# Attention row maxima turned by one VectorE block transpose a batch and taken ten heads ahead

## Chip, core and metric

The kernel runs on one core of one Trainium2 chip. The metric is the device time of one execution in microseconds (us), the median of the runs of that kernel. The engines are named as the profile names them: PE is TensorE's matmul and PEld its weight load, DVE is VectorE, ACT is ScalarE, POOL is GpSimd, SP is SyncE, which only issues transfers here.

## What is computed

One post-norm transformer layer on `x[32, 256, 128]`, 32 batches of 256 tokens. The attention has 16 heads of 8 features and a bias that falls linearly with the distance of query and key; the feed-forward part has four layers of width 512.

```python
def attention(x):                                   # wq, wk, wv, wo: 128 x 128
    q, k, v = heads(x @ wq.T), heads(x @ wk.T), heads(x @ wv.T)     # [32, 16, 256, 8]
    a = einsum('bhqd,bhkd->bhqk', q, k) / sqrt(8)
    a = softmax(a + slopes[h] * -abs(key - query), axis=-1)
    return merge(einsum('bhqk,bhkd->bhqd', a, v)) @ wo.T + bo

def ffn(x):                                         # ternary weights, scaled by column
    h = silu(lin(x, w1)) * lin(x, w2)
    h = gelu(lin(h, h1)); h = gelu(lin(h, h2))
    return lin(h, w3)

x = layernorm(x + attention(x)); x = layernorm(x + ffn(x))
```

## The kernel before

**Two parts.** `attention` works through the 32 batches, `ffn` through 16 chunks of 512 tokens after it. Only the attention part is touched. Every engine runs its own program in a fixed order, and semaphores tie them together. A step `t` stands for a batch; it has 16 slots `k`, one for each head. The program of every engine is laid out step by step and slot by slot, from step -4 to step 33.

**Each score matrix is made twice.** The softmax needs the maximum of each row before its exponent. So PE first computes the scores of a head with queries on the partitions into a bank `ps_a` (L464), and DVE takes the negated row maxima from it (L762, 128 rows x 2 blocks of queries) into `neg_sb`. Later PE computes the same scores with keys on the partitions into a bank `ps_b` (L472), with the maxima fed in as two more rows of the query operand `qk_stack`, and ACT takes the exponent into `probs` (L654). One slot does both for different heads: head `k` of batch `t` for the exponent, and for the maxima the head that stands `AHEAD = 4` heads further on (`a_slot`). In slots 0 to 11 of step `t` that is head 4 to 15 of batch `t + 1`, in slots 12 to 15 it is head 0 to 3 of batch `t + 2`. A slot's twelve matmuls (four L464, four L472, four of L479, which add the bias where query and key blocks meet) are called a **round** here.

**The way of a maximum.** The maxima have to come back as rows. After eight heads PE transposes half of `neg_sb` by a matmul with the identity into a `ps_b` bank (`turn_max`, L534), ACT copies 16 rows from it to `max_f` (`copy_max`, L630), POOL splits them into two bf16 parts `mrow` (`split_max`, L825 and L827), and SP sends each part into `qk_stack` (`max_rows`, L373). PE waits for that (`m_landed`) at slot 0 for heads 0 to 7, and at slot 8 for heads 8 to 15.

**What stands between the rounds.** The table `AT` says after which slot's round PE does what else: `wo` (L548) and `v` (L540) project, `turn o` (L562) transposes the attention output of the batch before into a `ps_a` bank, `turn norm` (L570) its normalised form into a `ps_b` bank, `qk` (L579) projects queries and keys of batch `t + 4`, and `pv 0` to `pv 3` (L523) multiply four heads' probabilities with the values. DVE has the row maxima in slot order and between them `add_residual` (L713), `take_stats` (L719), `normalise` (L743, L746) and `sum_stats` (L724).

**The banks.** All uses of `ps_a` take three banks in turn, in the order of the list `A_USES`: the 16 rounds with `wo` and `turn o` between them, 18 uses a step. A use waits until the one three places ahead of it in that list has been read: for a round's bank that is `max_done`, the end of DVE's reduction of that round. The uses of `ps_b` take four banks in the same way (`B_USES`, 21 a step, `max 0` and `max 1` among them), and wait for ACT's reading of the one four places ahead.

**The start.** Steps -4 to -1 fill the pipeline: there are projections and maxima, but no exponents before slot 0 of step 0. The maxima of batch 0 begin in slot 12 of step -2.

## Time and profile before

| | |
|---|---|
| median of 3 runs | 802.08 us (801.79 to 804.29) |
| profiled execution, its own time | 799.74 us |
| its span, first to last instruction | 797.9 us |
| busy PE, DVE, ACT, POOL | 96%, 79%, 77%, 39% of the span |
| attention part | about the first 440 us of the span |
| mean granted TensorE clock | 0.995 of full speed |

The span is 1.8 us shorter than the execution's own time, and that execution is 2.3 us below the median. The busy shares are means over two parts with different limits; the attention part is to be read by itself. In the timeline an instruction's matmuls overlap, so what a step of PE costs is the distance of its start from the start of the next, not its duration. The same holds for DVE's and ACT's instructions where they stand back to back.

### The profile page before, as it was taken

How to read it: one execution, taken by the hardware profiler on the slowest of the kernel's cores; microseconds unless marked ns; L12 is line 12 of the kernel's file. 1: busy time of each engine (PE TensorE's matmuls, PEld its weight loads, DVE VectorE, ACT ScalarE, POOL GpSimd, SP SyncE). 2: the span in 40 equal slices, each digit the busy share in tenths (PEclk: the TensorE clock that was granted, in tenths of full speed). 3: DMA queues.
4: the chain of work that ended last, by engine and by line, in shares of the span. 5: the costliest groups of instructions: out<-in, count | busy, mean ns of one | idle time of the engine just before them, and what ended most of it. 6: DMA issues, size and time to landing. Idle time of an engine off the chain costs nothing.

```text
span 797.9 us, 26869 instructions
## 1 busy us (share of the span) xinstructions
PE 769.2 (96%) x10370; PEld 557.4 (70%) x10370; DVE 630.1 (79%) x1303; ACT 611.7 (77%) x1096; POOL 313.4 (39%) x490
## 2 busy tenths in 40 slices
PE   4999999999999999999999999999999999999995
PEld 2566666666666666666665788888888888888873
DVE  4789899899989999989993767777777776666774
ACT  5588787888888888878878777777777777777762
POOL 5346878787756657575634200000000000000001
PEclk9999999999999999999999999999999999999998
DMA  6755565656556565564621100111111111101001
GB/s 181 190 145 166 168 185 159 195 151 182 164 159 166 141 181 136 170 174 144 174 65 44 41 27 28 39 41 39 39 39 39 31 34 39 39 26 40 16 26 54
DMA packets 107341, 81.37 MB, mean 102 GB/s; under 512 B 11168, under 2 KB 94112, under 8 KB 107232
## 3 DMA queue, kind: packets, MB, share of 16 engines
q1 hardware_dynamic: 105632, 76.59, 34.1%
q0 software_dynamic: 880, 2.88, 1.3%
q8 instruction: 79, 1.29, 0.7%
q10 hardware_dynamic: 720, 0.36, 0.2%
q14 instruction: 30, 0.25, 0.1%
HBM read 45.72 MB, written 33.55 MB: 99 GB/s over the span
## 4 chain that ended last, share of the span: by engine, by line
PE 92%; DVE 2%; DMA 2%; issue 2%; ACT 1%; POOL 1%; SPq 0%; POOLq 0%; ACTq 0%; DVEq 0%
PE ps_b L951 17%; PE ps_b L954 17%; PE ps_o L523 15%; PE ps_a L464 11%; PE ps_b L472 6%; PE ps_b L579 4%; PE ps_a L951 3%; PE ps_a L954 3%; PE ps_a L548 2%; PE ps_a L479 2%; PE ps_b L540 2%; PE ps_a L562 2%; PE ps_b L479 2%; PE ps_b L570 1%; PE ps_b L534 1%
## 5 line engine op out<-in xcount | busy, mean ns | idle before, releaser
L762 DVE TENSOR_REDUCE neg_sb<-ps_a 128x2 f32<-128x512 f32 x512 | 324.7, 681 | 37.1 <-PE ps_a L479 29.7
L654 ACT ACTIVATE probs<-ps_b 128x512 f32<-128x512 f32 x512 | 281.4, 591 | 57.2 <-PE ps_b L479 57.1
L464 PE MATMUL ps_a<-qk_stack 52*64 52x256 bf16 x2048 | 178.0, 281 | 5.6 <-DMA qk_stack<-qk_scratch 2.8
L472 PE MATMUL ps_b<-qk_stack 54*64 54x256 bf16 x2048 | 172.3, 276 | 1.1 <-ACT probs L654 0.9
L1062 ACT ACTIVATE gelu_f<-ps_b,sc 128x512 f32<-128x512 f32 x124 | 85.5, 690 | 74.0 <-PE ps_b L954 66.4
L464 PEld LDWEIGHTS ps_a<-qk_stack 52*64 52x64 bf16 x2048 | 82.5, 108 | 79.4 <-DVE neg_sb L762 61.0
L523 PE MATMUL ps_o<-probs,v_aug 128*32 128x256 f32 x2048 | 137.3, 385 | 0.0
L1224 POOL TENSOR_SCALAR vareps_f<-meanvar_f 128x4 f32<-128x4 f32 x15 | 9.7, 644 | 301.0 <-DVE meanvar_f L1125 301.0
L479 PE MATMUL ps_a<-corner_sb,eye_sb 64*64 64x128 bf16 x1024 | 116.4, 222 | 0.3 <-issue 0.3
L479 PE MATMUL ps_b<-corner_sb,eye_sb 64*64 64x128 bf16 x1024 | 114.4, 218 | 0.0
L951 PE MATMUL ps_b<-g2h,h_hi 128*128 128x512 f32 x256 | 102.7, 401 | 0.0
L951 PE MATMUL ps_b<-g1h,h_hi 128*128 128x512 f32 x256 | 101.6, 397 | 0.0
L954 PE MATMUL ps_b<-g1l,h_hi 128*128 128x512 f32 x256 | 101.5, 396 | 0.0
L954 PE MATMUL ps_b<-g2l,h_hi 128*128 128x512 f32 x256 | 101.4, 396 | 0.0
L1107 DVE TENSOR_TENSOR g2l<-gelu_f,g2h 128x512 fp32r<-128x512 f32 x64 | 44.3, 693 | 54.1 <-ACT g2h L1063 52.7
L472 PEld LDWEIGHTS ps_b<-qk_stack 54*64 54x64 bf16 x2048 | 81.0, 107 | 4.0 <-ACT probs L654 2.7
L523 PEld LDWEIGHTS ps_o<-probs,v_aug 128*32 128x32 f32 x2048 | 53.5, 109 | 41.6 <-issue 5.5
L1107 DVE TENSOR_TENSOR g3l<-gelu_f,g3h 128x512 fp32r<-128x512 f32 x64 | 42.8, 687 | 31.0 <-ACT g3h L1063 31.0
L479 PEld LDWEIGHTS ps_a<-corner_sb,eye_sb 64*64 64x64 bf16 x1024 | 59.0, 109 | 0.5
L479 PEld LDWEIGHTS ps_b<-corner_sb,eye_sb 64*64 64x64 bf16 x1024 | 57.7, 106 | 0.7 <-issue 0.5
L951 PEld LDWEIGHTS ps_b<-g1h,h_hi 128*128 128x128 f32 x256 | 48.3, 188 | 12.0 <-issue 0.2
L954 PEld LDWEIGHTS ps_b<-g1l,h_hi 128*128 128x128 f32 x256 | 48.2, 188 | 11.7
(124 smaller groups left out, 1429.3 us busy)
## 6 DMA issues: line engine op xcount, KB each, us to landing
qk_stack<-qk_scratch SPq DMA_DIRECT2D x128, 192.0 KB, 3.4
qk_scratch<-qk_sb SPq DMA_DIRECT2D x64, 192.0 KB, 3.0
qk_scratch<-qk_sb SPq DMA_DIRECT2D x96, 128.0 KB, 3.0
xT_sb<-in_xT SPq DMA_DIRECT2D x32, 128.0 KB, 3.5
x_sb<-in_x SPq DMA_DIRECT2D x32, 128.0 KB, 3.4
x_scratch<-x_sb SPq DMA_DIRECT2D x32, 128.0 KB, 3.4
x_in<-x_scratch SPq DMA_DIRECT2D x32, 128.0 KB, 2.1
x_res<-x_scratch SPq DMA_DIRECT2D x32, 128.0 KB, 2.1
```

The costliest lines, as they stand in the source:

```text
L464: pe.matmul(ps[side * TILE:(side + 1) * TILE, qb * SEQ:(qb + 1) * SEQ], q_stack[i][rows_of, j, at:at + TILE], k_stack[i][rows_of, j, :], s ...
L472: pe.matmul(ps[side * TILE:(side + 1) * TILE, kb * SEQ:(kb + 1) * SEQ], k_stack[i][rows_of, j, at:at + TILE], q_stack[i][rows_of, j, :], s ...
L479: return pe.matmul(out, eye_sb[rows_of, :], corner_sb[rows_of, 2 * turned + sub, :, :], start=False, stop=True, skip_group_check=True)
L523: mm = pe.matmul(ps_o[VCOLS * g:VCOLS * (g + 1), pack, :], v_flat[:, kb, first:first + VCOLS], probs[:, h % HALF, kb * SEQ:(kb + 1) * SEQ] ...
L540: mm = pe.matmul(ps[:, tb * D:(tb + 1) * D], xT_sb[t % XT_BUFS][:, tb * P:(tb + 1) * P], wv_sb[:], start=True, stop=True, skip_group_check ...
L579: mm = pe.matmul(ps[:, n * SEQ:(n + 1) * SEQ], w[:], xT_sb[(t + 4) % XT_BUFS][:], start=True, stop=True, skip_group_check=True)
L654: nc.scalar.activation(probs[:, h % HALF, :], ps_b[b_bank(t, k)][:], ACT.Exp, scale=slope[h]).then_inc(exp_done, 1)
L762: nc.vector.tensor_reduce(negmax[:, h_a // HALF, h_a % GROUPS, h_a % HALF // GROUPS, :], ps_a[a_bank(t, k)][:].rearrange("p (b k) -> p b k ...
L951: pe.matmul(ps[:], w_hi, a_hi, start=(k == 0), stop=False)
L954: return pe.matmul(ps[:], w_hi, a_lo, start=False, stop=(k == kt - 1))
L1062: nc.scalar.activation(gelu_f[:, o, :], ps_r[o][:], ACT.Gelu, scale=scale)
L1107: nc.vector.tensor_tensor(lo[:, o, :], gelu_f[:, o, :], hi[:, o, :].bitcast(F32), ALU.subtract).then_inc(signal, 1)
```

## The change

The maxima of all 16 heads of a batch now go as one piece. `neg_sb` shrinks to 128 x 32. When DVE has reduced head 15, it transposes `neg_sb` itself, block by block of 32 x 32, into `max_t` (`turn_max` on DVE). ACT moves the four blocks side by side into `max_f` (32 x 128) with four instructions after the exponent of slot 7 (`move_max`). POOL splits all 32 rows at once, and SP sends two transfers a batch where there were four. PE's two transposes, their `ps_b` banks and ACT's two copies are gone, and PE waits for `m_landed` at slot 0 alone. `AHEAD` becomes 10, and in `AT` the other entries are placed anew. Copying `v_aug` comes one slot later on ACT, `copy_oT` and the copy of `qk_f` stand after slot 12, `sum_stats` after slot 10, `normalise` after slot 7.

```diff
-AT = {"v": 1, "wo": 1, "pv 3": 4, "max 0": 6, "turn o": 6, "pv 0": 6, "turn norm": 8, "pv 1": 10, "qk": 13, "max 1": 13, "pv 2": 15}
-AHEAD = 4
+AT = {"v": 1, "wo": 1, "pv 3": 4, "turn o": 7, "pv 0": 7, "pv 1": 9, "turn norm": 12, "qk": 12, "pv 2": 15}
+AHEAD = 10
...
+def b_head(k):
+    return k ^ (AHEAD + 1) % 2
...
-        neg_sb = sb("neg_sb", [P, 2, P])
-        negmax = neg_sb[:, :, 0:BLK * HALF].rearrange("p n (g h a) -> p n g h a", g=GROUPS, h=HH)
-        max_f = [sb(f"max_f{i}", [BLK * HALF, P]) for i in range(2)]
-        mrow = [sb(f"mrow{i}", [BLK * HALF, MPARTS, P], BF16) for i in range(2)]
+        neg_sb = sb("neg_sb", [P, BLK * HEADS])
+        negmax = neg_sb.rearrange("p (g h a) -> p g h a", g=GROUPS, h=HG)
+        max_t = sb("max_t", [P, SQUARE])
+        max_f = sb("max_f", [BLK * HEADS, P])
+        mrow = sb("mrow", [BLK * HEADS, MPARTS, P], BF16)
...
 # SP
-            def max_rows(b, i, hf):
-                wait(sp, m_split, b * 2 + hf + 1)
+            def max_rows(b, i):
+                wait(sp, m_split, b + 1)
                 for r in range(MPARTS):
-                    dst = qk_stack[i][MROW + r:P:TILE, 0, hf * HH:(hf + 1) * HH, :]
-                    sp.dma_start(dst.rearrange("g h (b q) -> g (h b) q", b=BLK),
-                                 mrow[hf][:, r, :]).then_inc(m_landed[hf], DMA)
+                    dst = qk_stack[i][MROW + r:P:TILE, 0, :, :]
+                    sp.dma_start(dst.rearrange("g h (b q) -> g (h b) q", b=BLK), mrow[:, r, :]).then_inc(m_landed, DMA)
             def step(t, s):
-                if live(t, BATCH):
-                    max_rows(t, s, 1)
...
-                if live(t + 1, BATCH) and t >= -1:
-                    max_rows(t + 1, (s + 1) % STACKS, 0)
+                if live(t + 1, BATCH):
+                    max_rows(t + 1, (s + 1) % STACKS)
...
 # PE
-                    if k % HALF == 0:
-                        wait(pe, m_landed[k // HALF], (t + 1) * MPARTS * DMA)
+                    if k == 0:
+                        wait(pe, m_landed, (t + 1) * MPARTS * DMA)
...
-            def turn_max(t, hf):
-                wait(pe, max_done, (t + 1) * HEADS + (hf + 1) * HALF)
-                ps = take_b(t, f"max {hf}")
-                if t < 0:
-                    pe.wait_ge(neg_set, 1)
-                pe.transpose(ps[:, 0:P], neg_sb[:, hf, :], id_sb[:]).then_inc(mT_done, 1)
...
 # ACT
-            def copy_max(t, hf):
-                wait(act, mT_done, (t + 1) * 2 + hf + 1)
-                wait(act, m_split, t * 2 + hf + 1)
-                nc.scalar.activation(max_f[hf][:], ps_b[b_bank(t, f"max {hf}")][0:BLK * HALF, 0:P],
-                                     ACT.Copy).then_inc(m_copied, 1)
+            def move_max(b):
+                wait(act, m_turned, b + 1)
+                wait(act, m_split, b)
+                for n in range(QUADS):
+                    quad = slice(n * SQUARE, (n + 1) * SQUARE)
+                    nc.scalar.activation(max_f[:, quad], max_t[quad, :], ACT.Copy).then_inc(m_moved, 1)
...
+                    if k == 7 and live(t + 1, BATCH):
+                        move_max(t + 1)
...
 # DVE
+            def turn_max(b):
+                wait(dve, max_done, (b + 1) * HEADS)
+                wait(dve, m_moved, b * QUADS)
+                nc.vector.transpose(max_t[:], neg_sb[:]).then_inc(m_turned, 1)
...
-                        if h_a % HALF == 0:
-                            wait(dve, mT_done, b_a * 2 + h_a // HALF - 1)
+                        if h_a == 0:
+                            wait(dve, m_turned, b_a)
...
+                        if h_a == HEADS - 1:
+                            turn_max(b_a)
...
 # POOL
-                if live(t, BATCH):
-                    split_max(t, 1)
                 if live(t + 3, BATCH) and t + 3 > 0:
                     split_qk(t + 3, qk_sb[1 - par])
-                if t == -1:
-                    split_max(0, 0)
-                if live(t + 1, BATCH) and t >= 0:
-                    split_max(t + 1, 0)
+                if live(t + 1, BATCH):
+                    split_max(t + 1)
```

**PE at `turn o`**, before. The rows begin with the last two bias matmuls of slot 6; the digit after `ps_a` and `ps_b` is the bank.

```order
L479 MATMUL ps_a1<-corner_sb,eye_sb 64x2x64
L479 MATMUL ps_b2<-corner_sb,eye_sb 64x2x64
L534 MATMUL ps_b3<-id_sb,neg_sb 128x128 [waits exp_done,max_done]
L562 MATMUL ps_a2<-id_sb,o_sb 128x128 [waits max_done,o_copied]
L562 MATMUL ps_a2<-id_sb,o_sb 128x128 x3
L523 MATMUL ps_o<-probs,v_aug1 32x256 [waits exp_done,o_copied,v_copied]
L523 MATMUL ps_o<-probs,v_aug1 32x256 x7
L464 MATMUL ps_a0<-qk_stack0 64x256 [waits exp_done,max_done]
```

PE at the same place in the changed kernel, from the last two bias matmuls of slot 7.

```order
L480 MATMUL ps_a2<-corner_sb,eye_sb 64x2x64
L480 MATMUL ps_b1<-corner_sb,eye_sb 64x2x64
L556 MATMUL ps_a0<-id_sb,o_sb 128x128 [waits max_done,o_copied]
L556 MATMUL ps_a0<-id_sb,o_sb 128x128 x3
L524 MATMUL ps_o<-probs,v_aug1 32x256 [waits exp_done,o_copied,v_copied]
L524 MATMUL ps_o<-probs,v_aug1 32x256 x7
L465 MATMUL ps_a1<-qk_stack1 64x256 [waits exp_done,max_done]
```

The transpose of the maxima is gone from PE, and `turn o` moved behind one more round. Its bank was that of slot 4's round and is now that of slot 5's.

**DVE from the residual of a step to its `normalise`**, before.

```order
L713 TENSOR_TENSOR res<-ps_a,xb_sb 128x256 [waits x1_done,xb_done,wo_done]
L762 TENSOR_REDUCE neg_sb<-ps_a 128x2 [waits scores_a] x2
L762 TENSOR_REDUCE neg_sb<-ps_a 128x2 [waits scores_a,mT_done]
L719 BN_STATS bn<-res 128x6 [waits res_done]
L719 BN_STATS bn<-res 128x6
L762 TENSOR_REDUCE neg_sb<-ps_a 128x2 [waits scores_a] x2
L743 RECIPROCAL recip<-ps_a 128x32 [waits o_turned]
L746 TENSOR_TENSOR o_norm<-ps_a,recip 128x256 [waits recip_done,oT_done]
```

The same stretch of DVE in the changed kernel.

```order
L702 TENSOR_TENSOR res<-ps_a,xb_sb 128x256 [waits x1_done,xb_done,wo_done]
L756 TENSOR_REDUCE neg_sb<-ps_a 128x2 [waits scores_a] x3
L708 BN_STATS bn<-res 128x6 [waits res_done]
L708 BN_STATS bn<-res 128x6
L756 TENSOR_REDUCE neg_sb<-ps_a 128x2 [waits scores_a]
L742 STREAM_TRANSPOSE max_t<-neg_sb 128x32 [waits m_moved,max_done]
L756 TENSOR_REDUCE neg_sb<-ps_a 128x2 [waits scores_a,m_turned]
L756 TENSOR_REDUCE neg_sb<-ps_a 128x2 [waits scores_a]
L732 RECIPROCAL recip<-ps_a 128x32 [waits o_turned]
L735 TENSOR_TENSOR o_norm<-ps_a,recip 128x256 [waits recip_done,oT_done]
```

Slot 5's reduction is now the last of a batch. The transpose stands right behind it and waits for it (`max_done`), and slot 6's reduction, the first of the next batch, waits for the transpose (`m_turned`).

## Rows read from the trace of the kernel before

**Rows 1.** The page: span, and busy time, share, instructions of PE and DVE.
```profile
span 797.9 us, 26869 instructions
...
PE 769.2 (96%) x10370; PEld 557.4 (70%) x10370; DVE 630.1 (79%) x1303; ACT 611.7 (77%) x1096; POOL 313.4 (39%) x490
```

**Rows 2.** Waits, 200 to 400 us: who waited for whom, us, times, longest us.
```profile
PEld ps_a L464 <- DVE neg_sb L762: 29.2, 76, 0.4
```

**Rows 3.** Timeline of PE, one step: start us, us, engine, line, operation, count.
```profile
212.92 0.71 PE L548 MATMUL ps_a<-wo_sb,oT_sb 128*128 128x128 f32 x4
...
214.01 0.29 PE L464 MATMUL ps_a<-qk_stack 52*64 52x256 bf16 x1
...
214.97 1.07 PE L523 MATMUL ps_o<-probs,v_aug 128*32 128x256 f32 x16
215.97 0.29 PE L464 MATMUL ps_a<-qk_stack 52*64 52x256 bf16 x1
...
216.65 0.33 PE L534 MATMUL ps_b<-id_sb,neg_sb 128*128 128x128 f32 x1
216.81 0.60 PE L562 MATMUL ps_a<-id_sb,o_sb 128*128 128x128 f32 x4
217.34 1.07 PE L523 MATMUL ps_o<-probs,v_aug 128*32 128x256 f32 x16
218.35 0.29 PE L464 MATMUL ps_a<-qk_stack 52*64 52x256 bf16 x1
...
223.00 0.27 PE L534 MATMUL ps_b<-id_sb,neg_sb 128*128 128x128 f32 x1
223.20 0.29 PE L464 MATMUL ps_a<-qk_stack 52*64 52x256 bf16 x1
...
225.56 0.71 PE L548 MATMUL ps_a<-wo_sb,oT_sb 128*128 128x128 f32 x4
```

**Rows 4.** Timeline of DVE in that step, neighbours of one kind merged.
```profile
214.53 1.89 DVE L762 TENSOR_REDUCE neg_sb<-ps_a 128x2 f32<-128x512 f32 x3
216.33 0.47 DVE L719 BATCH_NORM_STATS2 bn<-res 128x6 f32<-128x128 f32 x2
216.72 1.27 DVE L762 TENSOR_REDUCE neg_sb<-ps_a 128x2 f32<-128x512 f32 x2
217.91 0.34 DVE L743 RECIPROCAL recip<-ps_a 128x32 f32<-128x32 f32 x1
218.36 0.42 DVE L746 TENSOR_TENSOR o_norm<-ps_a,recip 128x256 f32<-128x256 f32 x1
```

**Rows 5.** Groups by form, 100 to 420 us: count, busy us, mean ns, idle before.
```profile
L630 ACT ACTIVATE max_f<-ps_b 16x128 f32<-16x128 f32 x51 | 13.2, 259 | 8.2 <-PE ps_b L534 8.2
...
L743 DVE RECIPROCAL recip<-ps_a 128x32 f32<-128x32 f32 x25 | 8.6, 345 | 0.0
L724 DVE BATCH_NORM_AGGREGATE meanvar<-bn 128x2 f32<-128x6 f32 x50 | 5.9, 160 | 0.0
```

**Rows 6.** Timeline of the start of the maxima, DVE, PE, then PE's first exponent round.
```profile
16.99 3.68 DVE L762 TENSOR_REDUCE neg_sb<-ps_a 128x2 f32<-128x512 f32 x6 [3.62 <-PE ps_a L479]
...
17.73 0.64 PE L464 MATMUL ps_a<-qk_stack 52*64 52x256 bf16 x4 [0.25 <-DVE neg_sb L762]
...
30.91 0.42 PE L472 MATMUL ps_b<-qk_stack 54*64 54x256 bf16 x1
```

**Rows 7.** Timeline of ACT (exponents of slots 7 to 9) and of POOL, same step.
```profile
218.90 1.64 ACT L654 ACTIVATE probs<-ps_b 128x512 f32<-128x512 f32 x3 [0.18 <-PE ps_b L479]
...
217.34 0.28 POOL L825 CAST mrow<-max_f 16x128 bf16<-16x128 f32 x1 [0.28 <-ACT max_f L630]
217.71 0.42 POOL L827 TENSOR_TENSOR mrow<-max_f,mrow 16x128 bf16<-16x128 f32 x1
```

**Rows 8.** The page: transfers, KB each, us to landing; SP's issues at the start.
```profile
qk_stack<-qk_scratch SPq DMA_DIRECT2D x128, 192.0 KB, 3.4
...
10.05 0.52 SPq L358 DMA_DIRECT2D qk_scratch<-qk_sb  x1
12.18 1.75 SPq L366 DMA_DIRECT2D qk_stack<-qk_scratch  x4
```

More of the change, by code:

```diff
@@ L73 @@
 SPILLS = 5
+SQUARE = 32
 XT_BUFS = 6
+QUADS = P // SQUARE
 def slopes():
@@ L93, in wait_apart @@
         eng.sem_inc(passed, 1)
-AT = {"v": 1, "wo": 1, "pv 3": 4, "max 0": 6, "turn o": 6, "pv 0": 6, "turn norm": 8, "pv 1": 10, "qk": 13, "max 1": 13, "pv 2": 15}
-AHEAD = 4
+AT = {"v": 1, "wo": 1, "pv 3": 4, "turn o": 7, "pv 0": 7, "pv 1": 9, "turn norm": 12, "qk": 12, "pv 2": 15}
+AHEAD = 10
 STACKS = 4
 A_USES = [use for k in range(HEADS) for use in (k, *(n for n in ("wo", "turn o") if AT[n] == k))]
-B_USES = [use for k in range(HEADS) for use in (k, *(n for n in ("v", "max 0", "turn norm", "qk", "max 1") if AT[n] == k))]
+B_USES = [use for k in range(HEADS) for use in (k, *(n for n in ("v", "turn norm", "qk") if AT[n] == k))]
 A_BANKS, B_BANKS = 3, 4
@@ L143, in b_batch @@
 def b_batch(t, use):
-    return t + {"v": 0, "max 0": 1, "max 1": 1, "turn norm": -1, "qk": 4}[use] if isinstance(use, str) else t
+    return t + {"v": 0, "turn norm": -1, "qk": 4}[use] if isinstance(use, str) else t
 def last_use(t, use, uses, banks, batch, first):
@@ L301, in attention @@
         scores_a, max_done = sem("scores_a"), sem("max_done")
-        mT_done, m_copied, m_first, m_split = sem("mT_done"), sem("m_copied"), sem("m_first"), sem("m_split")
-        m_landed = [sem(f"m_landed{i}") for i in range(2)]
+        m_turned, m_moved, m_first, m_split, m_landed = sem("m_turned"), sem("m_moved"), sem("m_first"), sem("m_split"), sem("m_landed")
         scores_b, exp_done = sem("scores_b"), sem("exp_done")
@@ L453, in take_b @@
                         wait(pe, qk_copied, b + 1)
-                    elif isinstance(before[1], str):
-                        wait(pe, m_copied, b * 2 + int(before[1][-1]) + 1)
                     else:
@@ L467, in score_exp @@
             def score_exp(ps, i, k, kb, side):
[L469 removed]
+                h = b_head(k)
                 g, j = h % GROUPS, h // GROUPS
@@ L603, in step @@
                         project_v(t)
-                    if k == (5 if t < 0 else AT["max 0"]) and live(t + 1, BATCH):
-                        turn_max(t, 0)
                     if k == AT["turn o"] and live(t - 1, BATCH - 1):
@@ L611, in step @@
                         project_qk(t)
-                    if k == AT["max 1"] and live(t + 1, BATCH):
-                        turn_max(t, 1)
                     if k == AT["pv 3"] and live(t - 1, BATCH):
@@ L655, in step @@
                                              scale=slope[h]).then_inc(exp_done, 1)
-                    if k == 2 and live(t, BATCH):
+                    if k == 3 and live(t, BATCH):
                         wait(act, v_done, t + 1)
@@ L667, in step @@
                         nc.scalar.activation(o_sb[:], ps_o[:], ACT.Copy).then_inc(o_copied, 1)
[L668 to L673 removed]
+                    if k == 3 and t == -1:
+                        lay_rows(3, 0)
+                        lay_rows(3, 1)
+                    if k == 7 and live(t + 1, BATCH):
+                        move_max(t + 1)
+                    if k == 12 and live(t - 1, BATCH - 1):
                         copy_oT(t)
[L675 removed]
+                    if k == 12 and live(t + 4, BATCH):
                         wait(act, qk_done, t + 5)
@@ L679, in step @@
                                              ACT.Copy).then_inc(qk_copied, 1)
-                    if k == 14 and live(t + 1, BATCH):
-                        copy_max(t, 1)
                     if t < FIRST + 3 and k == 14:
@@ L772, in step @@
                         take_stats(t, par)
-                    if k == 11 and live(t - 2, BATCH):
+                    if k == 10 and live(t - 2, BATCH):
                         sum_stats(t, par)
-                    if k == 6 and live(t - 1, BATCH):
+                    if k == 7 and live(t - 1, BATCH):
                         normalise(t)
```

28 lines of the change are left out of this document (9 added, 19 removed).

## The prediction

> **What bounds the kernel now.** The page comes first: PE is busy 96% of the span, DVE 79% [rows 1]. Over the whole kernel that says little, so the second view is the timeline of PE over one step of the attention part [rows 3]. There the reader is to look at starts alone. From one `wo` to the next, 212.92 to 225.56, is 12.64 us, and each piece of PE's program begins as soon as the one before it has been streamed. Two rounds cost 0.68 us (215.97 to 216.65), three cost 0.96 us (214.01 to 214.97), so a round is 0.28 us and each group of rounds costs 0.12 us more. A `pv` is 1.00 us (214.97 to 215.97), `turn o` 0.53 us (216.81 to 217.34). PE's queue itself sets the step: what is taken from it shortens the step, unless a wait takes its place.
>
> The third view is DVE in the same step [rows 4]. Three reductions in 1.80 us (214.53 to 216.33) make 0.60 us each when they stand back to back, with the last result 0.69 us after its start, as two in 1.27 us also show. DVE's 16 reductions alone are 9.6 us of the step's 12.64. The waits [rows 2] name it as nearly the only thing that PE waits for: 76 times in 200 us PE's weight load stood ready for a bank that DVE was still reading. That costs nothing now, because the load stands behind the matmuls still streaming; it shows how little room there is.
>
> **What leaves PE.** The first transpose of the maxima holds the queue 0.16 us (216.65 to 216.81), the second 0.20 us (223.00 to 223.20), of which up to 0.10 us is the start of the round behind it and stays. `AT` now makes six groups of rounds of seven, which saves 0.12 us. `turn norm` now stands directly before `qk` instead of between two groups; that is worth nothing, or, if its start overlap is like that of `turn o`, 0.09 us. Together 0.38 us (0.16 + 0.10 + 0.12) to 0.57 us; I take 0.43 us, near the first, since that is read from starts and the rest is overlap. PE's own work is then 12.21 us a step.
>
> **The wait that takes its place.** `turn o` now stands behind the three rounds of slots 5 to 7, and its bank is the one that DVE empties with slot 5's reduction. PE's side: slot 2's round starts at 214.01, three rounds 0.96, `pv 3` 1.00, three rounds 0.96, so PE comes to `turn o` at 216.93 [rows 3]. DVE's side is there to read, for nothing before it changes: reductions of slots 2, 3, 4 from 214.53, then the two statistics instructions from 216.33, then slot 5's reduction from 216.72, finished 0.69 us later at 217.41 [rows 4]. DVE can't be earlier, because slot 2's reduction starts 0.52 us after its round, as soon as the round is done. How fast PE follows such an end is shown at the start of the kernel: the first reduction begins at 16.99 and ends 0.69 us later at 17.68, and PE, which waits for it, goes on at 17.73, after 0.05 us [rows 6]. So `turn o` starts at 217.46, a stall of 0.53 us. Bounds: 0.48 us if PE's restart overlaps, 0.60 us if the stream has to fill again. Before, the same bank belonged to slot 4's round, whose reduction ended at 216.42, 0.39 us ahead of `turn o` at 216.81.
>
> The net of a step is +0.10 us (0.53 - 0.43), between -0.09 (0.48 - 0.57) and +0.22 (0.60 - 0.38). It counts in the steps in which DVE has both maxima and the residual, 2 to 30: 29 steps, **+2.9 us**, between -2.6 and +6.4. In steps 0, 1 and 31 the saving stands with a small stall or none: **-0.5 us**.
>
> **DVE's new work.** The block transpose is not in the trace. The nearest rows by width are the 128x32 reciprocal, 345 ns, and by kind of cheapness the aggregation, 160 ns [rows 5]; I take 0.25 us between them. It also waits for the reduction before it, and the next reduction waits for it. `normalise` shows what such a wait costs: the reciprocal ends at 218.25, its reader starts at 218.36 [rows 4], 0.11 us, where unwaited reductions start 0.09 us before the end of the last. All of that lies behind the result that `turn o` waits for, and beside `turn o`, `pv 0` and the rounds after them. The first round that can notice is slot 9's, which takes slot 7's bank. PE gets there at 217.46 + 0.53 + 1.01 + 0.30 = 219.30 [rows 3]. DVE is through slot 7 at 217.41 + 0.11 + T + 0.11 + 0.60 + 0.69 = 218.92 + T, and 0.05 us later PE may go. So a transpose of up to 0.33 us is free, and the upper end of 0.345 costs 0.4 us in all. If that cover were gone, each 0.1 us would cost 2.9 us.
>
> The Trainium skill (VectorE: DVE Perf Modes, The DRAIN you can't avoid) says that chaining DVE instructions by semaphores costs nothing extra, eight copies taking 13.88 us either way. The row above disagrees by 0.20 us a wait. By the page the free length of the transpose would be about 0.7 us instead of 0.33 us, the sum would be the same, and the third rival below would have no ground.
>
> **ACT, POOL, SP.** ACT gives up two copies of 259 ns [rows 5] and gets four moves of a quarter of the width, at most as long: up to 0.5 us more in a step in which it already waits for PE before slot 7's exponent [rows 7]. POOL does one pair of 0.28 and 0.42 us instead of two [rows 7], SP two issues fewer. Nothing there is queued so that PE waits for it. What must be in time are the maxima at slot 0: exponent 7 starts at about 218.90 and holds ACT 0.5 us, four moves until 220.4, POOL until 221.2, the second issue at about 221.8, and slot 0 comes at 224.9 to 225.0. That leaves 3.1 us for landing. Landings shown are 3.4 us for 192 KB, and 2.13 us from an issue at 10.05 to what waited for it at 12.18 [rows 8]; a transfer of 8 KB on a queue with room is nearest to the second, so I take no cost. At 3.4 us it would be 0.3 us a step, 9 us.
>
> **The start.** The maxima of batch 0 begin when `qk_stack` lands, and the earlier slot number changes nothing on that. DVE's pace rules: six reductions in 3.68 us [rows 6], (3.68 - 0.69) / 5 = 0.60 us. Before the first exponent round at 30.91 [rows 6] 20 heads had gone through; now it must be 26. That is 6 x 0.60 = **+3.6 us**. It isn't given back at the end: the last ten rounds then have no maxima instead of the last four, but a round costs PE the same with or without them, since both kinds stream side by side, and PE is the bound.
>
> **Sum.** 3.6 + 2.9 - 0.5 = +6.0 us, so the profiled execution would take 799.74 + 6.0 = 805.7 us, of which 1.8 us lies outside the span, and the median 802.08 + 6.0 = **808.1 us**. With the bounds of the step the same case reaches from 802.6 to 811.6 us. A measurement of this kernel can tell about 0.3% from no change, 2.4 us: faster is below 799.7, slower above 804.5.
>
> **The rivals.**
> - *The saving arrives whole (faster).* If slot 5's reduction were out of the way when PE reaches `turn o`, only 0.43 us a step would be left: 29 x -0.43 - 0.5 + 3.6 = -9.4 us, **792.7 us**. It decides at 216.88: DVE would have to be 0.53 us earlier than its row says. For it speaks only that DVE has 3 us a step to spare in sum; against it that slot 2's reduction can't start before its round. Chance 0.12.
> - *The change just about cancels.* The overlaps all fall on PE's side: -0.09 us x 29 and the start, 3.6 - 2.6 - 0.5 = +0.5 us, **802.6 us**. A start that is hidden after all gives 802.08 + 2.9 - 0.5 = 804.5 us, the edge of the same. Chance 0.16.
> - *The block transpose is long.* From 0.33 us on it counts. At 0.48 us it adds 0.15 x 29 = 4.4 us: **812.5 us**. The 345 ns row speaks for the neighbourhood, the 160 ns row against it. Chance 0.12.
> - *The maxima come late at slot 0.* At a landing of 3.4 us 0.3 us a step: 6.0 + 9 = +15, **817 us**. The wait would stand ahead of PE's whole queue, and DVE and ACT would wait behind it. Chance 0.08.
> - *My forecast*, stall and start as read: 0.52.
>
> **Chances and range.** Slower: 0.52, of which 0.03 falls below 804.5, with 0.12 and 0.08, makes 0.69. Same: 0.14 of the cancelling case and the 0.03 make 0.17. Faster: 0.12 and 0.02 make 0.14. The range leaves out the first rival and the last: 800.5 to 813.5 us.
>
> **What would show it.** In the profile after: PE's start to start from `wo` to `wo` near 12.74 us; an idle row or a late start of about 0.5 us before `turn o` with DVE's row maxima as what ended it, in each step; the block transpose with 0.16 to 0.35 us; the first exponent round near 34.5 us; no wait for a transfer at slot 0. I am wrong if `turn o` follows slot 7's round after 0.38 us, if the first exponent round still starts near 31, or if the step is longer than 12.9 us, which would point to the transpose or the landing.

## The result, and the profile after

The changed kernel takes **806.34 us** in the median of 8 runs (805.20 to 807.84), the kernel before 801.46 us beside it (800.68 to 804.29): ratio 1.0063, 95% interval 1.0049 to 1.0077. It is slower by 4.9 us (0.6%), where 6.0 us were forecast. The profiled execution took 806.97 us, 7.2 us more than that of before (799.74 us).

The page of the changed kernel: span, busy times, then the head of the chain that ended last, by engine and by line.

```profile
span 805.1 us, 26576 instructions
...
PE 763.5 (95%) x10306; PEld 553.4 (69%) x10306; DVE 636.8 (79%) x1335; ACT 623.6 (77%) x1160; POOL 290.7 (36%) x425
...
PE 83%; DVE 12%; issue 2%; ACT 1%; DMA 1%; SPq 0%; POOL 0%; POOLq 0%; DVEq 0%; ACTq 0%
```

PE is busy 5.7 us less than in [rows 1], and the span is longer all the same. The second view says why: in the chain DVE has 12%, and in the kernel before it has 2% and PE 92%. The third view is PE's timeline over one step, the answer to [rows 3]: from `wo` to `wo`, some rows of the rounds left out.

```profile
296.38 0.71 PE L542 MATMUL ps_a<-wo_sb,oT_sb 128*128 128x128 f32 x4
...
297.47 0.29 PE L465 MATMUL ps_a<-qk_stack 52*64 52x256 bf16 x1
...
298.43 1.07 PE L524 MATMUL ps_o<-probs,v_aug 128*32 128x256 f32 x16
299.53 0.27 PE L465 MATMUL ps_a<-qk_stack 52*64 52x256 bf16 x1
...
301.00 0.63 PE L556 MATMUL ps_a<-id_sb,o_sb 128*128 128x128 f32 x4 [0.45 <-DVE neg_sb L756]
301.56 1.07 PE L524 MATMUL ps_o<-probs,v_aug 128*32 128x256 f32 x16
...
309.20 0.71 PE L542 MATMUL ps_a<-wo_sb,oT_sb 128*128 128x128 f32 x4
```

The step is 12.82 us instead of 12.64. `turn o` has an idle row of 0.45 us, released by DVE's row maxima; between 60 and 400 us there are 26 such waits, one a step, 10.9 us in all. Before, `turn o` waited there once, for 0.3 us, and not for DVE. The same stretch on DVE, the answer to [rows 4]:

```profile
297.99 1.89 DVE L756 TENSOR_REDUCE neg_sb<-ps_a 128x2 f32<-128x512 f32 x3
299.79 0.47 DVE L708 BATCH_NORM_STATS2 bn<-res 128x6 f32<-128x128 f32 x2
300.18 0.67 DVE L756 TENSOR_REDUCE neg_sb<-ps_a 128x2 f32<-128x512 f32 x1
300.89 0.21 DVE L742 STREAM_TRANSPOSE max_t<-neg_sb 128x32 f32<-128x32 f32 x1
301.13 1.29 DVE L756 TENSOR_REDUCE neg_sb<-ps_a 128x2 f32<-128x512 f32 x2
```

Slot 2's round starts at 297.47, its reduction 0.52 us later; three reductions, two statistics and slot 5's reduction follow without a gap until 300.85, and PE goes on at 301.00. The block transpose takes 0.21 us. A step without a stall takes these 12.82 us, but 12.89 us in steps 3 to 13, in which DVE has one more reduction of 0.68 us for the weights of the second part (L779). On ACT (the answer to [rows 7]):

```profile
298.99 0.39 ACT L652 ACTIVATE v_aug<-ps_b 128x256 f32<-128x256 f32 x1
299.57 0.60 ACT L658 ACTIVATE o_sb<-ps_o 128x512 f32<-128x512 f32 x1 [0.18 <-PE ps_o L524]
...
302.15 0.99 ACT L622 ACTIVATE max_f<-max_t 32x32 f32<-32x32 f32 x4
```

The four moves take 0.99 us together, where two copies of 259 ns stood before [rows 5]. No row of a step shows PE waiting for the maxima's transfer at slot 0. At the start (the answer to [rows 6]): DVE's reductions, PE's first exponent round, a wait in step 0, and `wo` of step 2.

```profile
24.89 2.49 DVE L756 TENSOR_REDUCE neg_sb<-ps_a 128x2 f32<-128x512 f32 x4 [0.24 <-PE ps_a L480]
...
35.06 0.42 PE L473 MATMUL ps_b<-qk_stack 54*64 54x256 bf16 x1
...
39.81 0.39 PE L465 MATMUL ps_a<-qk_stack 52*64 52x256 bf16 x1 [0.56 <-ACT v_aug L652]
...
63.03 0.71 PE L542 MATMUL ps_a<-wo_sb,oT_sb 128*128 128x128 f32 x4
```

The first exponent round starts 4.15 us later than before (30.91). In the kernel before `wo` of step 2 and of step 28 stand here:

```profile
57.38 0.71 PE L548 MATMUL ps_a<-wo_sb,oT_sb 128*128 128x128 f32 x4
...
390.91 0.71 PE L548 MATMUL ps_a<-wo_sb,oT_sb 128*128 128x128 f32 x4
```

So of the 7.2 us between the two profiled executions 4.15 us come before the first exponent, 1.50 us in steps 0 and 1 (63.03 - 57.38 = 5.65), and 2.44 us between the `wo` of steps 2 and 28 (399.00 - 390.91 = 8.09); 0.9 us is given back at the end. But 26 steps at 0.18 us would be 4.7 us. What is missing lies mostly in the kernel before: its 26 steps took 333.5 us, where 26 x 12.64 is 328.6. Of these 4.9 us, 0.35 us belong to step 15, which has two small matmuls more in both kernels, 0.8 us are two waits for a transfer of `xT_sb`, and most of the rest are stalls of PE of 0.1 to 1.3 us for which the profile names no releaser. The changed kernel's 26 steps are 2.65 us longer than 26 x 12.82: the same 0.35 us, 0.8 us in steps 3 to 13, and about 1.5 us of stalls.

The 1.50 us in steps 0 and 1 have to be read with TensorE's clock. e1_late_stats, which is described below, has the same program as the changed kernel up to step 2. Its granted clock, the column behind POOL, is 0.50 of full speed from 16 to 38 us, the lower of the two levels (1.2 and 2.4 GHz), and the bias matmuls last 0.31 us there and 0.22 us from 40 us on, where the granted clock is 1.00. In the changed kernel they last 0.31 us until 44.4 us:

```profile
16.00:38.00 22.00, 19.01 (x200) 11.64 (x204) 17.50 (x29) 7.65 (x10) 7.04 (x9) 0.50 0.83 205
```

```profile
L480 PE MATMUL ps_a<-corner_sb,eye_sb x70: 307/311/313, 16.7 to 43.9; 64*64 64x128 bf16 x70
```

The trace of the changed kernel has its first record of the clock at 44.8 us, and the views print 1.00 before it; the durations show that it was the lower level. In the kernel before the bias matmuls get short at 36 us. The first `pv` of step 0, in the changed kernel and in e1_late_stats:

```profile
41.55 1.93 PE L524 MATMUL ps_o<-probs,v_aug 128*32 128x256 f32 x16
```

```profile
40.83 1.07 PE L524 MATMUL ps_o<-probs,v_aug 128*32 128x256 f32 x16
```

From the first exponent round to `wo` of step 2 it is 27.98 us in the changed kernel, 26.34 us in e1_late_stats (35.12 to 61.46) and 26.47 us in the kernel before. So 1.64 us of the changed kernel's time there come with a clock that rose 5.8 us later, at 44.8 instead of 39.0 us. In e2_turn_twice it rose at 44.7 us and the stretch took 27.94 us, in e3_turn_four at 43.6 us and 27.30 us. Of the other executions of the changed kernel, the four with a mean granted clock of 0.978 or 0.979, which e1_late_stats also has in its profile, took 805.2 to 806.0 us, the two with 0.996, as in the profile of the changed kernel, 806.6 and 807.3 us, and one with 0.975 took 807.8 us. Why the clock rises earlier in one execution than in another, and whether the change itself delays it against the 36 us of the kernel before, no run shows.

### The profile page after: what moved, and what is told of

Read it like the earlier page. It is cut to its first block, busy times and chain, and to the rows that moved or that the text cites. A ratio compares the mean times of both kernels' runs of the same rounds, so it can differ in the third digit from the quotient of the medians.

```text
span 805.1 us, 26576 instructions
## 1 busy us (share of the span) xinstructions
PE 763.5 (95%) x10306; PEld 553.4 (69%) x10306; DVE 636.8 (79%) x1335; ACT 623.6 (77%) x1160; POOL 290.7 (36%) x425
## 4 chain that ended last, share of the span: by engine, by line
PE 83%; DVE 12%; issue 2%; ACT 1%; DMA 1%; SPq 0%; POOL 0%; POOLq 0%; DVEq 0%; ACTq 0%
PE ps_b L942 17%; PE ps_b L945 17%; PE ps_o L524 13%; DVE neg_sb L756 10%; PE ps_a L465 9%; PE ps_b L473 4%; PE ps_b L573 4%; PE ps_a L942 3%; PE ps_a L945 3%; PE ps_a L542 3%; PE ps_a L556 2%; PE ps_b L534 2%; PE ps_a L480 2%; PE ps_b L564 1%; PE ps_b L480 1%
## 5 line engine op out<-in xcount | busy, mean ns | idle before, releaser
L645 ACT ACTIVATE probs<-ps_b 128x512 f32<-128x512 f32 x512 | 271.1, 601 | 58.3 <-PE ps_b L480 58.2
L473 PE MATMUL ps_b<-qk_stack 54*64 54x256 bf16 x2048 | 169.4, 277 | 1.3 <-ACT probs L645 1.1
L465 PEld LDWEIGHTS ps_a<-qk_stack 52*64 52x64 bf16 x2048 | 85.0, 109 | 80.7 <-DVE neg_sb L756 52.3
L480 PE MATMUL ps_a<-corner_sb,eye_sb 64*64 64x128 bf16 x1024 | 118.1, 224 | 0.4 <-issue 0.4
L1215 POOL TENSOR_SCALAR vareps_f<-meanvar_f 128x4 f32<-128x4 f32 x15 | 5.4, 359 | 302.8 <-DVE meanvar_f L1116 302.8
L480 PEld LDWEIGHTS ps_a<-corner_sb,eye_sb 64*64 64x64 bf16 x1024 | 60.8, 110 | 0.8
```

The costliest lines, as they stand in the source:

```text
L465: pe.matmul(ps[side * TILE:(side + 1) * TILE, qb * SEQ:(qb + 1) * SEQ], q_stack[i][rows_of, j, at:at + TILE], k_stack[i][rows_of, j, :], s ...
L473: pe.matmul(ps[side * TILE:(side + 1) * TILE, kb * SEQ:(kb + 1) * SEQ], k_stack[i][rows_of, j, at:at + TILE], q_stack[i][rows_of, j, :], s ...
L480: return pe.matmul(out, eye_sb[rows_of, :], corner_sb[rows_of, 2 * turned + sub, :, :], start=False, stop=True, skip_group_check=True)
L645: nc.scalar.activation(probs[:, h % HALF, :], ps_b[b_bank(t, k)][:], ACT.Exp, scale=slope[h]).then_inc(exp_done, 1)
```

## The experiments

Theory W: PE's own saving arrives, and the time goes to three places, the wait of `turn o` for its bank, the longer start, and (added after the profile) ACT's copy of `v_aug`. Its rivals are named in the expectations. All times are medians, with the ratio to the kernel before on the same chip; the step is that of the steps without a stall.

| run | us | ratio, 95% interval | step, us | first exponent round |
|---|---|---|---|---|
| before | 801.5 | | 12.64 | 30.91 |
| changed | 806.34 | 1.0063, 1.0049 to 1.0077 | 12.82 | 35.06 |
| e1_late_stats | 803.02 | 1.0022, 1.0012 to 1.0032 | 12.69 | 35.12 |
| e2_turn_twice | 805.54 | 1.0050, 1.0031 to 1.0069 | 12.82 | |
| e3_turn_four | 805.29 | 1.0050, 1.0034 to 1.0066 | 12.82 | |
| e4_no_pe_turn | 797.15 | 0.9949, 0.9928 to 0.9969 | 12.52 | |
| e5_ahead8 | 815.71 | 1.0190, 1.0169 to 1.0211 | 13.11 | 33.39 |
| e6_late_v2 | 797.54 | 0.9961, 0.9947 to 0.9974 | 12.59 | 34.99 |
| e7_both8 | 804.50 | 1.0038, 1.0022 to 1.0054 | 12.63 | 33.13 |
| e8_both7 | 802.20 | 1.0006, 0.9992 to 1.0020 | 12.63, nine of 26 from 12.96 up | 32.04 |
| e9_move9 | 816.95 | 1.0189, 1.0173 to 1.0205 | 13.11 | 35.07 |
| e10_v2 | 804.03 | 1.0034, 1.0023 to 1.0046 | 12.82 | 35.29 |
| e11_both8_v2 | 800.27 | 0.9987, 0.9969 to 1.0004 | 12.54 | 33.09 |
| e12_late_v2_8 | 796.67 | 0.9938, 0.9925 to 0.9951 | 12.59 | 33.35 |

### The statistics out of the way: e1_late_stats

```diff
-                    if k == 4 and live(t - 2, BATCH):
+                    if k == 9 and live(t - 2, BATCH):
                         take_stats(t, par)
```

> The changed kernel with one thing moved: DVE's two statistics instructions stand after slot 9's reduction instead of after slot 4's. DVE's work in sum is the same. Theory W (the step is set by PE's program plus the wait before turn o for slot 5's reduction): the statistics take 0.39 us ahead of slot 5's reduction, so its result comes 0.39 us sooner and the wait of 0.45 us falls to about 0.06 us; the step goes from 12.82 us to between 12.43 and 12.65 us (the statistics now stand ahead of slot 10's reduction and can delay a bank there), 5 to 11 us less than the changed kernel. Theory S (DVE's work in sum sets the step): no change, 806 us, step 12.8 us.

3.3 us less than the changed kernel, and a step of 12.69 us: the direction is W's, the size is not. PE and DVE of this kernel:

```profile
306.84 1.07 PE L524 MATMUL ps_o<-probs,v_aug 128*32 128x256 f32 x16
307.94 0.27 PE L465 MATMUL ps_a<-qk_stack 52*64 52x256 bf16 x1
...
309.29 0.63 PE L556 MATMUL ps_a<-id_sb,o_sb 128*128 128x128 f32 x4 [0.32 <-DVE neg_sb L756]
```

```profile
308.45 0.69 DVE L756 TENSOR_REDUCE neg_sb<-ps_a 128x2 f32<-128x512 f32 x1 [0.16 <-PE ps_a L480]
```

Now DVE waits for slot 5's round (0.16 us) and `turn o` still waits for DVE: a round, its 0.52 us until the reduction, 0.69 us of reduction and 0.15 us until PE goes on are 1.35 us, and three rounds are only 0.96 us. A bank that is wanted three rounds after it was filled can't be had without a wait of 0.39 us, however idle DVE is. The other thing to see is `pv 3`: 1.10 us from 306.84 to 307.94, and 1.00 us before [rows 3].

### The length of the transpose: e2_turn_twice, e3_turn_four

```diff
+                for i in range(3):          # e2: range(1)
+                    nc.vector.transpose(max_x[i][:], neg_sb[:])
                 nc.vector.transpose(max_t[:], neg_sb[:]).then_inc(m_turned, 1)
```

> The changed kernel with the block transpose done twice in a row (the first into a tile that nobody reads). One takes 0.21 us, so DVE gets 0.12 to 0.21 us more a batch. Theory W: slot 7's result is there 0.37 us before slot 9's round asks for its bank, so this is free, within 0.5 us of the changed kernel. Theory S: 31 steps of 0.12 to 0.21 us, 4 to 6.5 us slower than the changed kernel.

> The changed kernel with the block transpose done four times in a row. DVE gets 0.36 to 0.63 us more a batch. Theory W: only what goes beyond 0.37 us counts, 0 to 0.26 us a step, 0 to 8 us slower than the changed kernel, and the wait shows ahead of slot 9's round. Theory S: 11 to 20 us slower.

One and three more transposes cost nothing in the step or the time. DVE of e3_turn_four:

```profile
298.82 0.67 DVE L759 TENSOR_REDUCE neg_sb<-ps_a 128x2 f32<-128x512 f32 x1
299.52 0.40 DVE L744 STREAM_TRANSPOSE max_x<-neg_sb 128x32 f32<-128x32 f32 x3
299.84 0.17 DVE L745 STREAM_TRANSPOSE max_t<-neg_sb 128x32 f32<-128x32 f32 x1
300.05 1.29 DVE L759 TENSOR_REDUCE neg_sb<-ps_a 128x2 f32<-128x512 f32 x2
```

From the reduction before them to the one behind them is 1.23 us with four and 0.95 us with one (300.18 to 301.13), so a transpose more is about 0.09 us when it waits for nothing. 0.28 us more in DVE's queue leaves the step at 12.82 us: DVE isn't saturated, and one late result of it is what PE waits for. That refutes theory S here and the "long transpose" of the prediction.

### PE without its two transposes: e4_no_pe_turn

The kernel before, with `turn_max` gone from PE and from `AT` and `B_USES`; ACT's `copy_max` writes zeros as the maxima's rows, so the exponents are taken without them and the output isn't the reference's.

```diff
-                nc.scalar.activation(max_f[hf][:], ps_b[b_bank(t, f"max {hf}")][0:BLK * HALF, 0:P],
-                                     ACT.Copy).then_inc(m_copied, 1)
+                nc.scalar.activation(max_f[hf][:], neg_sb[0:BLK * HALF, hf, :],
+                                     ACT.Copy, scale=0.0).then_inc(m_copied, 1)
```

> The kernel before (maxima four heads ahead) without PE's two transposes of the maxima and their two banks. The row maxima are taken and waited for as before, but the rows that go into qk_stack are zeros, so the exponents are of other values; the shapes, instructions and transfers are the same. Theory W: the step is PE's program, so it falls by 0.16 us and by 0.10 to 0.20 us, from 12.63 to 12.27 to 12.37 us, 8 to 11 us faster than the kernel before. Theory S: DVE sets the step, so nothing is gained.

4 us faster than before, and 0.12 us a step, less than half of what was expected.

```profile
302.72 0.29 PE L462 MATMUL ps_a<-qk_stack 52*64 52x256 bf16 x1
...
303.50 0.66 PE L553 MATMUL ps_a<-id_sb,o_sb 128*128 128x128 f32 x4
304.09 0.64 PE L521 MATMUL ps_o<-probs,v_aug 128*32 128x256 f32 x8
```

Two rounds and then `turn o` are 0.78 us here, 0.10 us more than two rounds last elsewhere. What `turn o` waits for is ACT's copy of `o_sb`, which it transposes; its weight load (PEld) and that copy:

```profile
303.50 0.20 PEld L553 LDWEIGHTS ps_a<-id_sb,o_sb 128*128 128x128 f32 x2 [0.26 <-ACT o_sb L656]
```

```profile
302.86 0.60 ACT L656 ACTIVATE o_sb<-ps_o 128x512 f32<-128x512 f32 x1 [0.18 <-PE ps_o L521]
```

The copy ends at 303.46 and `turn o` starts 0.05 us later, while DVE had emptied its bank at 303.16. So the first transpose had filled a wait for ACT. In the changed kernel, where `turn o` stands one round further from `pv 3`, that copy ends at 300.17 and `turn o` starts at 301.00, so this wait is gone. `turn o` then holds the queue 0.59 us and not 0.53, `qk`'s second half 0.52 us and not 0.43. So the two transposes, 0.36 us by their starts, were worth 0.12 us in their old place.

### Fewer heads ahead, and the place of the moves: e5_ahead8, e9_move9

```diff
-AHEAD = 10
+AHEAD = 8                      # not in e9_move9
...
-                    if k == 7 and live(t + 1, BATCH):
+                    if k == 9 and live(t + 1, BATCH):
                         move_max(t + 1)
```

> The changed kernel with AHEAD 8 instead of 10 and the four moves of the maxima after the exponent of slot 9 instead of slot 7. Theory P (the start is paced by DVE's row maxima, 0.60 us a head): 24 heads instead of 26 go through before the first exponent round, which starts at 35.06 - 1.2 = 33.9 us; turn o still waits for slot 5's reduction, so the step stays 12.82 us; the median is 1.2 us under the changed kernel's, 805.1 us. Rival L (the maxima now land too late): they are sent two slots and a pv later, some 1.7 us; in the changed kernel the last issue ends 3.2 us before slot 0's round, so 1.5 us would be left. With the 3.4 us of the landing shown for 192 KB slot 0 would wait 1.9 us in each of 31 steps, with the 2.13 us seen at the start (from the start of the issue) not at all. L gives 860 us, P 805.

> The changed kernel, AHEAD 10, with the four moves of the maxima after the exponent of slot 9 instead of slot 7. In e5_ahead8 the step was 13.11 us, not 12.82, with qk 0.30 us late behind turn norm, waiting for ACT's exponents. Theory A (the place of the moves does it): the moves hold ACT 0.98 us just ahead of slot 10's exponent, whose ps_b bank qk takes; then AHEAD plays no part, the step is 13.1 us here too, and the first exponent round stays at 35.0 us: about 806.3 + 29 x 0.29 = 814.7 us. Rival B (e5_ahead8 lost its time by AHEAD 8, by later landings or another order of the heads): the step stays 12.82 us and the time 806.3 us.

Both theories of e5 were wrong about the time. The first exponent round comes 1.67 us earlier (1.2 expected), but the step is 13.11 us. PE and ACT of e5_ahead8:

```profile
307.30 0.44 PE L564 MATMUL ps_b<-id_sb,o_norm 128*128 128x128 f32 x2
307.93 0.67 PE L573 MATMUL ps_b<-xT_sb,wqs_sb 128*128 128x256 f32 x2 [0.19 <-ACT probs L645]
```

```profile
306.32 0.98 ACT L622 ACTIVATE max_f<-max_t 32x32 f32<-32x32 f32 x4
307.21 1.52 ACT L645 ACTIVATE probs<-ps_b 128x512 f32<-128x512 f32 x3
```

`qk` follows `turn norm` after 0.63 us, not 0.33, and waits for the exponent of slot 10, which stands behind the moves. e9_move9 has AHEAD 10 and only the moves at slot 9, and its step is 13.11 us too, with the same 0.63 us: theory A. For the step it is the moves' place alone, and 0.30 us a step of ACT's work came onto PE's path. Rival L of e5 shows itself once:

```profile
61.37 0.27 PE L465 MATMUL ps_a<-qk_stack 52*64 52x256 bf16 x1 [1.78 <-DMA qk_stack<-mrow]
```

e9_move9 has an idle row of 1.70 us before the same round (at 65.11), for which the profile names no releaser. The maxima can be late, then, in an early step and with 1.7 us less room, and not in the later ones.

### The copy of v_aug: e6_late_v2, e10_v2

```diff
-                    if k == 3 and live(t, BATCH):
+                    if k == 2 and live(t, BATCH):
                         wait(act, v_done, t + 1)
```

e10_v2 has this alone, e6_late_v2 has the edit of e1_late_stats with it.

> e1_late_stats with ACT's copy of v_aug back after the exponent of slot 2, where the kernel before has it. In the changed kernel and in e1_late_stats pv 3 holds PE 1.10 us where the kernel before shows 1.00 us. Theory V: slot 5's round takes the ps_b bank that v was projected into, and since the copy of v_aug stands one slot later, ending at 312.20, the round starts at 312.31 instead of 312.24. With the statistics out of the way slot 5's round counts in full, so the step falls from 12.69 to 12.59 us, 29 x 0.10 = 2.9 us: 800.1 us. Rival R: what held the round was a bank of ps_a, as the row's releaser (row maxima) says; then nothing changes: 12.69 us and 803.0 us.

> The changed kernel with the copy of v_aug after slot 2's exponent again, and nothing else. Theory C (turn o's wait covers it): DVE's chain from slot 2's round over the statistics to slot 5's reduction sets turn o, so slot 5's round 0.10 us earlier is worth nothing in a step: 12.82 us; in step 0 the wait of 0.56 us for v_aug goes. About 805.8 us. Rival F (the two costs are independent): 12.72 us and 803 us, and then the 5.5 us between e1_late_stats and e6_late_v2 would be v_aug's alone.

The step of e6_late_v2 is 12.59 us, as theory V has it, and the time is 797.54 us, 3.5 us below the kernel before. PE of e6_late_v2:

```profile
303.94 1.07 PE L524 MATMUL ps_o<-probs,v_aug 128*32 128x256 f32 x16
304.94 0.29 PE L465 MATMUL ps_a<-qk_stack 52*64 52x256 bf16 x1
```

`pv 3` is back to 1.00 us. In e10_v2 the step stays 12.82 us (theory C): `pv 3` gives 0.10 us back and the idle row before `turn o` grows from 0.45 to 0.55 us.

```profile
295.93 1.07 PE L524 MATMUL ps_o<-probs,v_aug 128*32 128x256 f32 x16
296.93 0.29 PE L465 MATMUL ps_a<-qk_stack 52*64 52x256 bf16 x1
...
298.51 0.63 PE L556 MATMUL ps_a<-id_sb,o_sb 128*128 128x128 f32 x4 [0.55 <-DVE neg_sb L756]
```

Of its gain of 2.3 us most lies before the steps: `wo` of step 2 starts at 61.37, 1.66 us earlier than in the changed kernel, without the 0.56 us wait of step 0. But the clock also rose earlier here, at 41.4 and not 44.8 us. Between e1_late_stats and e6_late_v2, which differ by the copy of `v_aug` alone and whose clocks both rose at 39.0 us, it is 0.42 us (61.46 and 61.04). So the late copy costs 0.4 us before the steps, and the rest of the 1.66 us goes with the clock. In the steps the late statistics alone bring 29 x 0.13 = 3.8 us, the copy alone nothing, and both together 29 x 0.23 = 6.7 us; by the medians it is 3.3, 2.3 and 8.8 us. The 0.10 us of `v_aug` in each step shows only once `turn o` no longer hides it.

### turn o on a later bank: e7_both8, e8_both7, e11_both8_v2

```diff
-AT = {... "turn o": 7, "pv 0": 7, "pv 1": 9, "turn norm": 12, "qk": 12, "pv 2": 15}
+AT = {... "turn o": 8, "pv 0": 7, "pv 1": 9, "turn norm": 11, "qk": 12, "pv 2": 15}
-AHEAD = 10
+AHEAD = 8                      # e8_both7: 7
...
-                    if k == 10 and live(t - 2, BATCH):
+                    if k == 11 and live(t - 2, BATCH):
                         sum_stats(t, par)
-                    if k == 7 and live(t - 1, BATCH):
+                    if k == 8 and live(t - 1, BATCH):
                         normalise(t)
```

All three also have the moves at slot 9, and e11_both8_v2 the copy of `v_aug` at slot 2.

> e5_ahead8 with turn o behind slot 8's round, so that its bank is that of slot 6's, normalise after slot 8, turn norm after slot 11, sum_stats after slot 11. Theory W (what the change costs in a step is only the wait of turn o for its bank, 0.61 us): slot 6's reduction ends 3.98 us after slot 2's round starts, PE comes to turn o after 4.42 us, so the wait is gone. Two more groups of rounds cost 0.24 us: the step is 12.21 + 0.24 = 12.45 us, up to 12.5, and with the start of e5 the time is 805.1 - 29 x 0.35 = 795.0 us, under both kernels. Rival D (DVE is full): its work in such a step is 16 x 0.60 + 2.2 = 11.8 us, and 0.6 us more in the eleven steps that also count weight pieces; then a wait elsewhere takes the place of this one, the step is 12.6 us, 12.9 in the eleven: about 801 us.

> e7_both8 with AHEAD 7: one head less at the start, and the last of a batch is slot 8's reduction, still moved after the exponent of slot 9. If the start is paced at 0.60 us a head and the maxima still land in time: first exponent round at 33.3 us, 0.6 us under e7_both8. Rival L: the transpose behind slot 8's reduction ends some 0.8 us later than behind slot 7's, ACT reaches the moves later by part of it, and slot 0 waits for the transfer: each 0.1 us of wait is 3.1 us, so at 0.3 us 9 us over e7_both8.

> e7_both8 with the copy of v_aug after slot 2's exponent. In e7_both8 turn o waited for nothing and the step was 12.63 us. Theory Q (PE's own queue sets that step, with 0.10 us for v_aug in it): 12.53 us, 29 x 0.10 = 2.9 us less, 801.6 us. Rival: another wait ends just behind it, and the step stays 12.63 us, 804.5 us.

The wait of `turn o` is gone in e7_both8. PE of it, `pv 0` to `pv 1`:

```profile
310.19 1.07 PE L524 MATMUL ps_o<-probs,v_aug 128*32 128x256 f32 x16
311.19 0.29 PE L465 MATMUL ps_a<-qk_stack 52*64 52x256 bf16 x1
...
311.60 0.66 PE L556 MATMUL ps_a<-id_sb,o_sb 128*128 128x128 f32 x4
312.19 0.29 PE L465 MATMUL ps_a<-qk_stack 52*64 52x256 bf16 x1
...
312.58 1.07 PE L524 MATMUL ps_o<-probs,v_aug 128*32 128x256 f32 x16
```

But the step is 12.63 us, not 12.45: a round alone costs 0.40 us, so two more groups are 0.24 us; `v_aug` is 0.10 us; `turn o` (0.59 us) and `turn norm` (0.37 us) cost 0.03 and 0.04 us more where a round follows them. 12.21 + 0.24 + 0.10 + 0.07 = 12.62. It is 12.63 us in the steps with weight pieces too, so DVE isn't the bound (rival D). e11_both8_v2 takes away the 0.10 us: 12.54 us, theory Q. The times are worse than the steps say. In e7_both8 slot 0's round waits 0.91 us (at 48.69) and 1.89 us (at 62.99) for the maxima, and its later stalls, most without a releaser, come to about 3 us. e8_both7 starts its exponents 1.1 us earlier than e7_both8 and shows no wait for the transfer, so that its rival L fails; but nine of its 26 steps take 12.96 us or more. What they lose lies at different places (0.33 us behind `turn o` in the step at 293.9, 0.95 us at a `pv` in that at 74.7), and its cause is open.

### The version that beats both: e12_late_v2_8

```diff
 # e6_late_v2 with
-AHEAD = 10
+AHEAD = 8
```

> e6_late_v2 with AHEAD 8, the moves left after slot 7's exponent. The last maximum of a batch is then slot 7's. In e6_late_v2 slot 5's reduction ends at 306.14, so slot 7's ends at 307.34 and the transpose at 307.6, and ACT comes to the moves at 307.65. Theory P: nothing moves in the step, 12.59 us, and the first exponent round is at 33.3 us as in e5_ahead8, 1.7 us earlier: 795.9 us. Rival L: the moves slip behind the transpose, the maxima land later, and in the early steps, where e5_ahead8 and e7_both8 waited 0.9 to 1.9 us for their landing, the gain is lost again: 797.5 us or more.

796.67 us, 4.5 us (0.6%) below the kernel before and 9.7 us below the changed one. The first exponent round comes at 33.35, 1.64 us earlier than in e6_late_v2, the step stays 12.59 us, and ACT's moves find the transpose done (DVE, then ACT):

```profile
307.32 0.21 DVE L742 STREAM_TRANSPOSE max_t<-neg_sb 128x32 f32<-128x32 f32 x1
```

```profile
307.60 0.98 ACT L622 ACTIVATE max_f<-max_t 32x32 f32<-32x32 f32 x4
```

Against e6_late_v2 the median gains 0.9 us of the 1.6. Rival L shows itself in a small way: slot 0's round waits 0.27 us at 59.32 for the maxima's transfer, and by `wo` of step 2 1.04 us of the 1.64 are left. The intervals of the two ratios overlap, so this last step isn't settled. That both beat the kernel before is.

## Why the prediction was right, step by step

**PE's own saving, 0.43 us: right.** From slot 2's round to `turn o` PE's own work is 0.96 + 1.00 + 0.96 = 2.92 us and it took 3.53 us (297.47 to 301.00). The rest of the step, 12.82 - 3.53 = 9.29 us, and 2.92 make 12.21 us, the predicted number. Piece by piece the rows give the same: 0.36 us for the transposes, 0.12 for one group less and 0.04 for `turn norm` directly before `qk`, less 0.03 us by which `turn o` and 0.07 us by which `qk` hold the queue longer, are 0.42 us. What the prediction didn't see is that the first transpose in its old place filled a wait of `turn o` for ACT's copy of `o_sb`; e4_no_pe_turn, where this wait comes out, gets 0.12 us. That `turn o` also moved one round away from `pv 3` is what lets the whole 0.16 us arrive, and the prediction has no word on it: the number was right there by luck.

**The wait before `turn o`, 0.53 us: right in place and cause, too small by 0.08 us.** It is 3.53 - 2.92 = 0.61 us. The DVE chain was read as it came (3.40 us predicted from slot 2's round to the end of slot 5's reduction, 3.38 measured). The term that was off is how fast PE follows: 0.05 us, taken from a round at the start [rows 6]. `turn o` follows 0.15 us after the reduction's end, in the changed kernel (300.85 to 301.00) and in e10_v2 (298.36 to 298.51); why it takes 0.10 us more than a round isn't shown. The stated bound of 0.60 us was nearly it. Net +0.18 us a step instead of +0.10.

**The block transpose, 0.25 us: 0.21 us, free as said.** The self-waits were priced at 0.11 us each, from the reciprocal and its reader [rows 4]. They are 0.04 us (300.85 to 300.89) and 0.03 us (301.10 to 301.13), so with the overlap of 0.09 us that an unwaited reduction has, 0.12 to 0.13 us each instead of 0.20. The Trainium skill (VectorE: DVE Perf Modes, The DRAIN you can't avoid) says that a semaphore between DVE instructions costs nothing extra; this trace lies between that and the price taken. Either would have given the same time, since e3_turn_four has 0.28 us more there for nothing.

**ACT, POOL, SP: one sentence was wrong.** "Nothing there is queued so that PE waits for it" overlooked that the copy of `v_aug` frees the bank of slot 5's round. Moved behind one more exponent, it delays that round by 0.10 us in each step, which the wait of `turn o` covered, and costs 0.4 us before the steps (e1_late_stats against e6_late_v2). The +1.50 us of steps 0 and 1, where the sum has -0.5 us, are mostly the clock, which the prediction didn't have at all: with it at full from 39.0 us on, and the late copy in place, e1_late_stats takes 26.34 us for them, 0.13 us less than the kernel before, and e6_late_v2 without it 26.04 us (34.99 to 61.04), 0.43 us less, which is about the -0.5 us. The four moves were priced at up to 0.5 us more than the copies they replace (0.99 against 0.52 us), and that holds; e9_move9 shows how near they stand to PE's path.

**The start, +3.6 us: +4.15 us.** Six heads at DVE's pace were right; the transpose's own time in DVE's queue (0.95 - 0.60 = 0.35 us) was left out, and a pause of 0.24 us for PE more stands in the rows. e5_ahead8 and e12_late_v2_8 confirm the direction from the other side: two heads less bring 1.67 and 1.64 us, more than the 1.2 us of two heads at 0.60 us; one pause of 0.24 us fewer is part of the difference, and the rest is open.

**The sum.** 4.15 + 1.50 + 29 x 0.18 = 10.9 us would have missed by more than +6.0 did. Two things took from it: the last steps gave back 0.9 us, against the prediction's "isn't given back", and the kernel before lost more to stalls than the changed one, so that 26 steps cost 2.44 us and not 4.7. That leaves 4.15 + 1.50 + 2.44 - 0.92 = 7.2 us, the distance of the two profiled executions, of which 1.6 us go with the late clock. The prediction took the step of before as 12.64 us throughout, when its mean over 26 steps was 12.83 us. So the closeness of 6.0 to 4.9 us is in part luck: errors that cancel. Of the rivals, the whole saving (792.7 us) needed DVE to be earlier; e1_late_stats shows that even with the statistics gone 0.39 us of wait remains. The late maxima didn't occur in the steps.

## What to carry to other kernels

A bank used in rotation should be asked for no sooner than one round, the reader's latency and its length after it was filled; here that is 1.35 us, and an operation that takes PE's place between rounds must stand that far behind. When a copy is moved by one slot, look up which bank it frees and who wants that next, even where the copying engine has time to spare. Remove one wait and test the next at once: two edits worth 3.3 and 2.3 us were worth 8.8 us together, and turned a loss of 0.6% into a gain of 0.4%, with a shorter start 0.6%. Before a microsecond at the start of a kernel is put down to an edit, compare how long the same matmul takes in both traces: here 1.6 us were the clock's.
